# A two-layer perceiver block: the second query product moved behind the first scores, and two low parts of the experts exchanged

## The chip, the core and the metric

The kernel runs on one core of one Trainium2 chip. The time is that of one execution on the device in microseconds, from the first to the last instruction with what lies around them; of several runs the median counts.

## What is computed

Input are x (4 blocks of 128 rows, width 512) and a context (4 × 2048 rows, width 512). Six stages follow one another, each adding its result to x after a layer norm of its input:

```
x = x + cross attention, layer 0 (norm(x), ctx, ctx, mask)     # 16 heads of 32
x = x + retention, layer 0
x = x + experts, layer 0                                       # 8 experts, the best 2 of each row
x = x + norm(cross attention, layer 1 (norm(x), ctx, ctx))     # 16 heads of 32, no mask
x = x + gated recurrence, layer 1
x = x + experts, layer 1: 8 experts, the best 2 of each row:
        down(silu(gate(x)) * up(x)), weighted by the softmax of the two router values
```

The change touches cross attention (both layers use one function) and the experts of layer 1. In cross attention, q = norm(x) Wq + bq, k = ctx Wk + bk, v = ctx Wv + bv, scores = q k / sqrt(32) (where the mask hides a column, it counts as −1e9), softmax over the 2048 keys, times v, times Wo.

## The kernel before

**Cross attention, `stage_cross`.** All 512 queries (4 blocks of 128) are projected once, turned: product o (`project_q(o)`, L356) gives the 128 columns of q that belong to 4 heads, for all 512 rows, in one PSUM bank, `QB[o]`. It is a product in float32, from `wqT` (Wq, which lies in the tile `pt`) and `xT`. VectorE (`keep_q`, L578) adds the bias, in layer 0 also multiplies by a tile that clears fully hidden rows (four instructions), and splits the result into a high part `qhi` and a low part `qlo`; the semaphore `q_done` counts finished query blocks. Keys and values come in 16 groups of 512 keys: `project_k(g, o)` and `project_v(g, n)` use three products each of high and low parts (`three_products`, L91 to L95). Input of a group is split by ScalarE (`chi`, `high_part`) and GpSimd (`clo`, `low_part` L292).

Work is cut into 64 units u of four heads and one group: `scores(u)` (L399, twelve matmuls into the four banks S), maxima on VectorE (`max_of`: L605 with mask, L608 without), exponentials on ScalarE (L813), transposes of the probabilities (`turn_p`, L414, into two banks TB), copies to `pt`, and `outputs` (L431, into the bank `OB`) two units later. Keys and values run two units ahead. The order of each engine is written out by hand. Of TensorE's it is, ahead of the units:

```
v(0,0) v(0,1) turn_x k(0,0) [turn the mask's tile, layer 0] q(0) k(0,1) q(1)
unit 0: scores(0) q(2) v(0,2) q(3) k(0,2)      unit 1: scores(1) v(0,3) turn_p(0,0..1) k(0,3) turn_p(0,2..3)
```

VectorE's is `keep_q(0)`, `low_k(0, 1)`, `keep_q(1)`, then the four maxima of unit 0, `keep_q(2)`, `keep_q(3)`, the low part of k(0,2). The scores of unit 0 wait for two query blocks (`max(u + 1, 2)`, L405), though they read one. GpSimd starts on the second group's low parts when two query blocks are done (L315), and SyncE's load of the next group follows these. The bank OB is first written by the outputs of unit 0, in unit 2.

**Experts of layer 1, `stage_experts` with `layer` 1.** Rows are sorted into 15 tiles of 128 rows of one expert. Each tile g needs three weight matrices of 1 MB (kinds 0 gate, 1 up, 2 down) that SyncE loads into four slots in the order gate g, up g, down g − 1 (`load`, L1442). A slot is free once the low part of what was in it is made (`lo_done`). ScalarE makes the high part of a matrix (`high`, L1727), VectorE the low part (`low`, L1902 to L1905, 128 × 2048 elements). Rows of a tile are turned by TensorE (`turn_x`), their high part `xThi` made by ScalarE (`high_x`, L1740), the low part `xTlo` by VectorE (`low_x`, L1995). The gate product `expand(GB, 0, g)` (L1650) waits for `lo_done[0]` and `xlo_done` of its tile. Per pass g, the orders are:

```
TensorE: gate(g)  turn_h(g-1)  turn_x(g+1)  up(g)  contract(g-1)
ScalarE: silu(g)  high part of h(g-1)  high(gate, g+1)  high_x(g+1)  high(up, g+1)  high(down, g)  keep output
VectorE: low part of h(g-1)  low_x(g+1)  low(gate, g+1)  silu * up (g)  low(up, g+1)  low(down, g)
```

A wait in the text is a wait on a semaphore; an engine runs its instructions in order, so what is behind a waiting one waits too.

Of the kernel before, what the change touches and what calls it, by code (L numbers as in the profile page):

```python
# [27 lines left out]
C = D // P  # L28
# [146 lines left out]
def stage_cross(nc, k, name, t, L, x, x_in, mask, norm, prefetch):  # L175
# [19 lines left out]
    with ExitStack() as ctx:  # L195
# [34 lines left out]
        q_made, q_done, x_ready = sem("q_made"), sem("q_done"), sem("x_ready")  # L230
# [8 lines left out]
        S, TB, OB, KV = ps[0:4], ps[4:6], ps[6], ps[7]  # L239
        QB = (S[2], S[3], OB, TB[1])  # L240
        HALF = C * D // 2
# [12 lines left out]
        with nc.Block() as block:  # L254
# [35 lines left out]
            def _(pool):  # L290
# [23 lines left out]

                pool.wait_ge(q_done, 2)  # L315
                for c in range(C):
# [3 lines left out]
                for u in range(U + 2):  # L320
# [4 lines left out]
                    g = u // C  # L325
# [22 lines left out]
            def _(pe):  # L348
# [7 lines left out]
                def project_q(o):  # L356
                    pe.wait_ge(xT_done, C)
                    pe.wait_ge(wq_in, 16)
                    if o == 3:
                        pe.wait_ge(q_done, 1)  # L360
                        pe.wait_ge(v_done, 2)
                    for c in range(C):
                        last = pe.matmul(QB[o][:], wqT[:, c, o * P:(o + 1) * P], xT[:, c, :], start=(c == 0), stop=(c == C - 1))
                    last.then_inc(q_made, 1)
# [34 lines left out]
                def scores(u):  # L399

                    g, o = u // C, u % C
                    b = g // NCH
                    pe.wait_ge(klo_done, C * g + o + 1)
                    if u < C:
                        pe.wait_ge(q_done, max(u + 1, 2))  # L405
                    after(pe, exp_done, HPT * u)
                    for i, (q_part, k_part) in enumerate(((qhi, khi), (qhi, klo), (qlo, khi))):
                        for h in range(HPT):
                            rows = slice(h * HD, (h + 1) * HD)
                            ins = pe.matmul(S[h][:], q_part[rows, o, b * P:(b + 1) * P], k_part[rows, g % 2, o, :],  # L410
                                            start=(i == 0), stop=(i == 2))
                            if i == 2:
                                ins.then_inc(s_made, 1)

                def turn_p(u, n):
# [3 lines left out]
                    if u == 0 and n == 0:  # L419
                        pe.wait_ge(v_done, 2)  # L420
                    if u == 0 and n == 1:
                        pe.wait_ge(q_done, C)
# [8 lines left out]
                def outputs(u):  # L431
# [5 lines left out]
                    if u == 0:  # L437
                        pe.wait_ge(q_done, C - 1)
                    after(pe, oc_done, u)
# [54 lines left out]
                project_k(0, 1)  # L494
                project_q(1)
                for u in range(U + 2):
                    g, o = (u + C - LAG) // C, (u + C - LAG) % C
                    ahead = g < G
                    if u < U:
                        scores(u)  # L500
                    if u == 0:
                        project_q(2)
                    if 2 <= u < U + 2:
# [27 lines left out]
            def _(dve):  # L531
# [174 lines left out]
                low_k(0, 1)  # L706
                keep_q(1)
                if masked:
                    dve.wait_ge(hidden_done, 1)
                for u in range(U + 2):  # L710
# [5 lines left out]
                    if u == 0:  # L716
                        keep_q(2)
                        keep_q(3)
                    if u == U:
# [602 lines left out]
def stage_experts(nc, k, name, t, x, x_out, xg, od, layer, prefetch):  # L1322
# [30 lines left out]
    with ExitStack() as ctx:  # L1353
# [84 lines left out]
        with nc.Block() as block:  # L1438
# [440 lines left out]
            def _(dve):  # L1879
# [179 lines left out]
                else:  # L2059
                    for g in range(NG + 1):  # L2060
                        if g >= 1:
                            dve.wait_ge(hhi_done, g)
                            nc.vector.tensor_tensor(hlo[:, (g - 1) % 2, :], TB[0][:], f32(hhi[:, (g - 1) % 2, :]), ALU.subtract) \
                                .then_inc(hlo_done, 1)
                        if 1 <= g < NT - 1:
                            low_x(g + 1)
                        if g + 1 < NG:
                            low(0, g + 1)
                        if g < NG:
# [351 lines left out]
```

## Time and profile before

| what | value |
|---|---|
| three runs | 2252.75, 2248.92, 2246.71 us, median 2248.92 |
| the profiled execution | 2253.44 us |
| its span, first to last instruction | 2251.7 us |
| mean granted clock of TensorE | 0.969 |
| busy: TensorE, VectorE, ScalarE, GpSimd | 2120.6, 1410.6, 1376.8, 296.0 us |
| cross attention of layer 0 and of layer 1, about | 0 to 655 us, 1330 to 1970 us |
| experts of layer 1, about | 2058 us to the end |

The profile is one execution. Its page gives busy time of the engines and the costliest groups of instructions; its trace gives each instruction with start and length, what ended the idle time before it, and windows with busy time, granted clock and use of the DMA engines. Matmuls are pipelined: one starts before the one before it has ended, so the distance of two starts, not the length, is what one costs.

### The profile page before, as it was taken

What the parts mean: (1) busy time and instruction counts of PE and PEld (TensorE: products, weight loads), DVE (VectorE), ACT (ScalarE), POOL (GpSimd) and SP (SyncE); (2) the same over time, 40 slices, a digit from 0 to 9 for tenths busy, and PEclk for the clock granted to TensorE, in tenths of its full rate; (3) what the DMA queues carried; (4) which work ended last, traced back from release to release, by engine and by line L of the source; (5) the groups of instructions that cost most, each with busy time, mean ns of one, the idle gap of its engine ahead of it and who ended that gap; (6) DMA issues with size and microseconds to landing.
All of it is one profiled execution on the core that took longest, in us unless ns stands there. A gap on an engine that the chain in (4) does not pass through costs nothing. (4 is left out here: it accounts for less than half of the span.)

```text
span 2251.7 us, 37885 instructions
## 1 busy us (share of the span) xinstructions
PE 2120.6 (94%) x14773; PEld 1635.5 (73%) x14773; DVE 1410.6 (63%) x2399; ACT 1376.8 (61%) x2644; POOL 296.0 (13%) x268
## 2 busy tenths in 40 slices
PE   6999999999988987799999989999999999977998
PEld 4777787777864655688888856777877787756776
DVE  5555455555554775499999954555455454577887
ACT  3666566566652543388888835665665666554774
POOL 1111112122110000100000201121111121101001
PEclk9999999999997998899999989999999999988999
DMA  4001001010103012599999930100101010012996
GB/s 159 20 20 39 20 22 37 20 38 20 39 20 147 1 38 97 213 366 373 365 358 359 370 107 20 39 20 21 37 20 39 20 39 20 20 57 97 357 360 242
DMA packets 53776, 262.07 MB, mean 116 GB/s; under 512 B 9560, under 2 KB 9944, under 8 KB 26976
## 3 DMA queue, kind: packets, MB, share of 16 engines
q1 hardware_dynamic: 47296, 244.45, 29.0%
q0 software_dynamic: 2560, 8.39, 1.1%
q10 hardware_dynamic: 3744, 6.82, 0.8%
q8 instruction: 119, 1.95, 0.4%
q14 instruction: 57, 0.47, 0.1%
HBM read 243.65 MB, written 15.99 MB: 115 GB/s over the span
## 5 line engine op out<-in xcount | busy, mean ns | idle before, releaser
L613 DVE COPY c_pt<-bank 128x512 f32<-128x512 f32 x256 | 177.1, 692 | 557.5 <-PE bank L428 557.4
L813 ACT ACTIVATE c_pr<-wide,c_nmax 128x512 f32<-128x512 f32 x512 | 349.3, 697 | 147.5 <-DVE c_nmax L605 76.8
L295 POOL TENSOR_TENSOR c_clo<-land,c_chi 128x512 fp32r<-128x512 f32 x120 | 154.5, 1290 | 1007.0 <-ACT c_chi L782 911.9
L428 PE MATMUL bank<-ident,c_pr 128*128 128x128 f32 x2048 | 268.1, 274 | 2.7 <-ACT c_pt L820 1.4
L428 PEld LDWEIGHTS bank<-ident,c_pr 128*128 128x128 f32 x2048 | 239.8, 141 | 37.1 <-DVE c_pt L613 2.3
L796 ACT ACTIVATE c_khi<-bank,c_cols 128x512 fp32r<-128x512 f32 x128 | 88.1, 688 | 252.2 <-PE bank L95 252.2
L93 PE MATMUL bank<-c_wv_hi,c_chi 128*128 128x512 f32 x512 | 217.7, 425 | 18.4 <-DVE c_clo L544 17.1
L93 PE MATMUL bank<-c_chi,c_wk_hi 128*128 128x512 f32 x512 | 214.0, 418 | 0.3 <-DVE c_wk_lo L536 0.2
L94 PE MATMUL bank<-c_wv_lo,c_chi 128*128 128x512 f32 x512 | 202.6, 396 | 0.0
L95 PE MATMUL bank<-c_chi,c_wk_lo 128*128 128x512 f32 x512 | 202.4, 395 | 0.0
L95 PE MATMUL bank<-c_wv_hi,c_clo 128*128 128x512 f32 x512 | 202.3, 395 | 0.0
L94 PE MATMUL bank<-c_clo,c_wk_hi 128*128 128x512 f32 x512 | 199.1, 389 | 0.0
L820 ACT COPY c_pt<-bank 128x512 f32<-128x512 f32 x256 | 150.5, 588 | 63.0 <-PE bank L428 62.8
L605 DVE CUSTOM_DVE_ANT_0 wide<-wide,land 128x512 f32<-128x512 f32 x256 | 169.1, 722 | 5.8 <-PE wide L410 5.4
L608 DVE TENSOR_REDUCE c_nmax<-wide 128x1 f32<-128x512 f32 x256 | 158.8, 682 | 4.9 <-PE wide L410 4.6
L1905 DVE TENSOR_TENSOR moe_wlo<-moe_hr,moe_whi 128x2048 fp32r<-128x2048 f32 x68 | 153.3, 2284 | 6.7 <-ACT moe_whi L1732 6.7
L93 PE MATMUL wide<-moe_whi,moe_xThi 128*128 128x512 f32 x360 | 144.3, 401 | 10.0 <-issue 4.8
L95 PE MATMUL wide<-moe_whi,moe_xTlo 128*128 128x512 f32 x360 | 141.9, 394 | 0.0
L93 PEld LDWEIGHTS bank<-c_wv_hi,c_chi 128*128 128x128 f32 x512 | 96.7, 189 | 62.1 <-issue 24.3
L94 PE MATMUL wide<-moe_wlo,moe_xThi 128*128 128x512 f32 x360 | 141.6, 393 | 0.0
L444 PE MATMUL bank<-c_pt,c_v 128*32 128x128 f32 x4096 | 139.7, 278 | 1.6 <-ACT c_pt L820 1.6
L444 PEld LDWEIGHTS bank<-c_pt,c_v 128*32 128x32 f32 x4096 | 105.2, 110 | 49.5 <-issue 47.3
(416 smaller groups left out, 4270.1 us busy)
## 6 DMA issues: line engine op xcount, KB each, us to landing
moe_hr<-in_L_ffn_w SPq DMA_DIRECT2D x68, 1024.0 KB, 7.5
land<-in_L_ffn_w SPq DMA_DIRECT2D x34, 1024.0 KB, 7.8
land<-in_ctx SPq DMA_DIRECT2D x31, 1024.0 KB, 4.9
moe_raw<-in_L_ffn_w SPq DMA_DIRECT2D x18, 1024.0 KB, 7.8
moe_raw<-in_L_ffn_we_gate SPq DMA_DIRECT2D x8, 1024.0 KB, 6.8
land<-in_L_ffn_we_up SPq DMA_DIRECT2D x8, 1024.0 KB, 6.6
moe_raw<-in_L_ffn_we_down SPq DMA_DIRECT2D x8, 1024.0 KB, 6.7
moe_raw<-in_L_ffn_we_up SPq DMA_DIRECT2D x7, 1024.0 KB, 7.4
```

Of the source, the lines that this page charges most:

```text
L93: pe.matmul(out, w_hi, m_hi, start=start, stop=False, skip_group_check=not check)
L94: pe.matmul(out, w_hi, m_lo, start=False, stop=False, skip_group_check=not check)
L95: return pe.matmul(out, w_lo, m_hi, start=False, stop=stop, skip_group_check=not check)
L295: nc.gpsimd.tensor_tensor(clo[:, g % 2, c, :], raw[:, c, :], f32(chi[:, g % 2, c, :]), ALU.subtract) \
L428: last = pe.transpose(TB[n % 2][:, h * P:(h + 1) * P], pr[:, u % 2, h, n * P:(n + 1) * P], k["ident"][:])
L444: last = pe.matmul(OB[h * HD:(h + 1) * HD, 0:P], v[:, (T4 * g + n) % VR, at:at + HD], pt[:, n, h * P:(h + 1) * P], start=(n == 0), stop=(n ...
L605: nc.vector.tensor_tensor_reduce(S[h][:], S[h][:], hidden[:, i * CH:(i + 1) * CH], -1.0, BIG, ALU.add, ALU.min, into).then_inc(max_done, 1)
L608: nc.vector.tensor_reduce(into, S[h][:], AX.X, ALU.max, negate=True).then_inc(max_done, 1)
L613: nc.vector.tensor_copy(pt[:, n, :], TB[0][:]).then_inc(pt_dve, 1)
L813: nc.scalar.activation(pr[:, u % 2, h, :], S[h][:], ACT.Exp, bias=nmax[:, b % 2, i, at:at + 1], scale=-1.0 if masked else 1.0, accum_out=d ...
L820: nc.scalar.copy(pt[:, n, :], TB[1][:]).then_inc(pt_act, 1)
L1905: nc.vector.tensor_tensor(wlo[kind][:, g % 2, :], raw[n % RW], f32(whi[kind][:, g % 2, :]), ALU.subtract).then_inc(lo_done[kind], 1)
```

## The change

In `stage_cross`: product 1 of the queries goes behind the scores of unit 0 on TensorE, and its VectorE work behind the maxima of unit 0. Scores of unit 0, and GpSimd's first low parts, wait for one query block instead of two. The banks of the products become S[2], OB, TB[1], TB[0] in place of S[2], S[3], OB, TB[1]. The waits that go with the banks move: products 1 to 3 wait for one query block and the first two value blocks, the transposes of unit 0 for all four query blocks already at the first, the outputs of unit 0 for two blocks instead of three. In `stage_experts`, layer 1: in passes 1 to 13, VectorE makes the low part of the next gate weights ahead of that of the next rows.

```diff
--- before.py
+++ after.py
@@ -237,7 +237,7 @@
         done, acc_scaled, early_scaled, early_joined, late_joined = (sem(s) for s in ("done", "acc_scaled", "early_scaled", "early_joined", "late_joined"))
         ps = k["ps"]
         S, TB, OB, KV = ps[0:4], ps[4:6], ps[6], ps[7]
-        QB = (S[2], S[3], OB, TB[1])
+        QB = (S[2], OB, TB[1], TB[0])
         HALF = C * D // 2
         FIRST = 2 if x_in is not None else 1
         landings = list(k["landings"])
@@ -312,7 +312,7 @@
                     pool.wait_ge(scaled, 2 * n + 2)
                     nc.gpsimd.tensor_tensor(acc[:, b % 2, :], acc[:, b % 2, :], part[:, i % 2, :], ALU.add).then_inc(joined, 1)
 
-                pool.wait_ge(q_done, 2)
+                pool.wait_ge(q_done, 1)
                 for c in range(C):
                     low_part(1, c)
                 pool.wait_ge(q_done, C)
@@ -356,7 +356,7 @@
                 def project_q(o):
                     pe.wait_ge(xT_done, C)
                     pe.wait_ge(wq_in, 16)
-                    if o == 3:
+                    if o > 0:
                         pe.wait_ge(q_done, 1)
                         pe.wait_ge(v_done, 2)
                     for c in range(C):
@@ -402,7 +402,7 @@
                     b = g // NCH
                     pe.wait_ge(klo_done, C * g + o + 1)
                     if u < C:
-                        pe.wait_ge(q_done, max(u + 1, 2))
+                        pe.wait_ge(q_done, u + 1)
                     after(pe, exp_done, HPT * u)
                     for i, (q_part, k_part) in enumerate(((qhi, khi), (qhi, klo), (qlo, khi))):
                         for h in range(HPT):
@@ -417,8 +417,6 @@
                     if n == 0:
                         pe.wait_ge(exp_done, HPT * u + HPT)
                     if u == 0 and n == 0:
-                        pe.wait_ge(v_done, 2)
-                    if u == 0 and n == 1:
                         pe.wait_ge(q_done, C)
                     if n % 2 == 0:
                         after(pe, pt_dve, 2 * u + n // 2)
@@ -435,7 +433,7 @@
                     pe.wait_ge(pt_act, 2 * u + 2)
                     pe.wait_ge(v_done, T4 * g + T4)
                     if u == 0:
-                        pe.wait_ge(q_done, C - 1)
+                        pe.wait_ge(q_done, 2)
                     after(pe, oc_done, u)
                     after(pe, aT_done, C * finished(TURN, u + 2))
                     for n in range(T4):
@@ -492,13 +490,13 @@
                     pe.transpose(TB[1][:, 0:P], manyr, k["ident"][:]).then_inc(any_turned, 1)
                 project_q(0)
                 project_k(0, 1)
-                project_q(1)
                 for u in range(U + 2):
                     g, o = (u + C - LAG) // C, (u + C - LAG) % C
                     ahead = g < G
                     if u < U:
                         scores(u)
                     if u == 0:
+                        project_q(1)
                         project_q(2)
                     if 2 <= u < U + 2:
                         outputs(u - 2)
@@ -704,7 +702,6 @@
                     s.then(nc.vector.tensor_copy(manyT, TB[1][:, 0:P]))
                 keep_q(0)
                 low_k(0, 1)
-                keep_q(1)
                 if masked:
                     dve.wait_ge(hidden_done, 1)
                 for u in range(U + 2):
@@ -714,8 +711,8 @@
                         for h in range(HPT):
                             max_of(u, h)
                     if u == 0:
-                        keep_q(2)
-                        keep_q(3)
+                        for c in range(1, C):
+                            keep_q(c)
                     if u == U:
                         fold_max(G - 1)
                     if o == 2 and u > C and 0 < (g - 1) % NCH and g < G:
@@ -2062,10 +2059,10 @@
                             dve.wait_ge(hhi_done, g)
                             nc.vector.tensor_tensor(hlo[:, (g - 1) % 2, :], TB[0][:], f32(hhi[:, (g - 1) % 2, :]), ALU.subtract) \
                                 .then_inc(hlo_done, 1)
+                        if g + 1 < NG:
+                            low(0, g + 1)
                         if 1 <= g < NT - 1:
                             low_x(g + 1)
-                        if g + 1 < NG:
-                            low(0, g + 1)
                         if g < NG:
                             dve.wait_ge(up_made, g + 1)
                             dve.wait_ge(silu_done, g + 1)
```

## Rows read from the trace of the kernel before

**Rows 1.** The page: TensorE over the span, and VectorE's masked maxima

```profile
PE 2120.6 (94%) x14773; PEld 1635.5 (73%) x14773; DVE 1410.6 (63%) x2399; ACT 1376.8 (61%) x2644; POOL 296.0 (13%) x268
...
L605 DVE CUSTOM_DVE_ANT_0 wide<-wide,land 128x512 f32<-128x512 f32 x256 | 169.1, 722 | 5.8 <-PE wide L410 5.4
```

**Rows 2.** Windows, layer 0's attention: length, busy PE, PEld, DVE, ACT, POOL, clock, DMA

```profile
57.00:200.00 143.00, 142.61 (x1270) 113.90 (x1273) 75.34 (x193) 88.40 (x210) 29.60 (x24) 1.00 0.07 23
```

**Rows 3.** Timeline of TensorE, layer 0: start us, length us, engine, line, instruction

```profile
32.45 3.60 PE L363 MATMUL wide<-c_pr,c_pt 128*128 128x512 f32 x8
39.17 0.80 PE L410 MATMUL wide<-c_khi,c_qhi 32*128 32x512 f32 x4 [3.12 <-DVE c_qlo L587]
...
40.75 6.09 PE L363 MATMUL bank<-c_pr,c_pt 128*128 128x512 f32 x8
46.28 0.80 PE L93 MATMUL bank<-c_wv_hi,c_chi 128*128 128x512 f32 x1
...
49.43 3.59 PE L363 MATMUL bank<-c_pr,c_pt 128*128 128x512 f32 x8
52.46 0.79 PE L93 MATMUL bank<-c_chi,c_wk_hi 128*128 128x512 f32 x1
```

**Rows 4.** Timeline of VectorE, layer 0

```profile
32.16 0.69 DVE L587 TENSOR_TENSOR c_qlo<-c_v,c_qhi 128x512 fp32r<-128x512 f32 x1
...
38.33 0.69 DVE L587 TENSOR_TENSOR c_qlo<-c_v,c_qhi 128x512 fp32r<-128x512 f32 x1
```

**Rows 5.** Timeline of TensorE, head of layer 1's attention

```profile
1349.47 3.59 PE L363 MATMUL wide<-c_pr,c_pt 128*128 128x512 f32 x8
1355.26 0.51 PE L410 MATMUL wide<-c_khi,c_qhi 32*128 32x512 f32 x4 [2.20 <-DVE c_qlo L587]
...
1356.16 5.40 PE L363 MATMUL bank<-c_pr,c_pt 128*128 128x512 f32 x8
1361.00 0.79 PE L93 MATMUL bank<-c_wv_hi,c_chi 128*128 128x512 f32 x1
```

**Rows 6.** Timeline of VectorE, head of layer 1's attention

```profile
1348.26 0.69 DVE L587 TENSOR_TENSOR c_qlo<-c_v,c_qhi 128x512 fp32r<-128x512 f32 x1
```

**Rows 7.** Windows of 1 us, head of layer 0's attention

```profile
43.00:44.00 1.00, 1.00 (x2) 0.34 (x1) 0.64 (x2) 1.00 (x5) 1.00 (x1) 0.50 0.00 0
```

**Rows 8.** Timeline of GpSimd, layer 0

```profile
39.11 4.96 POOL L295 TENSOR_TENSOR c_clo<-land,c_chi 128x512 fp32r<-128x512 f32 x4 [37.42 <-DVE c_qlo L587]
```

**Rows 9.** Timeline of TensorE, experts of layer 1

```profile
2093.48 0.47 PE L93 MATMUL wide<-moe_whi,moe_xThi 128*128 128x512 f32 x1 [0.62 <-DVE moe_xTlo L1997]
...
2193.95 0.39 PE L95 MATMUL bank<-moe_whi,moe_hlo 128*128 128x512 f32 x1
2194.45 0.47 PE L93 MATMUL wide<-moe_whi,moe_xThi 128*128 128x512 f32 x1
...
2222.71 0.47 PE L93 MATMUL wide<-moe_whi,moe_xThi 128*128 128x512 f32 x1
```

**Rows 10.** Timeline of VectorE, experts of layer 1

```profile
2191.45 0.69 DVE L1997 TENSOR_TENSOR moe_xTlo<-bank,moe_xThi 128x512 fp32r<-128x512 f32 x1 [0.93 <-ACT moe_xThi L1740]
2192.06 2.28 DVE L1905 TENSOR_TENSOR moe_wlo<-moe_raw,moe_whi 128x2048 fp32r<-128x2048 f32 x1
```

**Rows 11.** Timeline of ScalarE, experts of layer 1

```profile
2189.01 1.94 ACT L1732 CAST moe_whi<-moe_raw 128x2048 fp32r<-128x2048 f32 x1
2190.82 0.60 ACT L1740 CAST moe_xThi<-bank 128x512 fp32r<-128x512 f32 x1
```

**Rows 12.** Waits in the experts of layer 1: us in total, times, longest us

```profile
DVE moe_xTlo L1997 <- ACT moe_xThi L1740: 17.8, 15, 2.7
...
PE wide L93 <- issue: 3.1, 3, 1.5
PE wide L93 <- DVE moe_wlo L1905: 2.2, 1, 2.2
```

**Rows 13.** Windows of 2 us, experts of layer 1 (columns as in rows 2)

```profile
2114.00:2116.00 2.00, 2.00 (x9) 1.63 (x10) 2.00 (x2) 2.00 (x2) 0.00 (x0) 1.00 0.64 164
```

## The prediction

> **What bounds the kernel now.** I read the page first: TensorE is busy for 94% of the span and no other engine for more than 63% [rows 1]. That is a mean, so I went to the stretches in which the changed lines run. In the body of an attention stage TensorE is busy 142.61 of 143 us at full clock and VectorE 75.34 [rows 2]: there TensorE alone sets the time, and whatever its queue reaches earlier stays won until the stage ends. The head of the stage is different. The timeline of TensorE [rows 3] shows a hole: the second query product starts at 32.45, and then the engine stands idle 3.12 us until the first scores start at 39.17. VectorE's timeline [rows 4] names the cause: the low part of the second query block (start 38.33, 0.69 long) ends at 39.02, and the scores wait for two blocks though unit 0 reads only the first, which was ready at 32.85. The third query product, right behind the hole, takes from 40.75 to 46.28, 5.53 us, where the fourth takes 3.03 (49.43 to 52.46). A look at the granted clock says why: 0.50 in that stretch [rows 7], the lower of TensorE's two levels, 1.2 instead of 2.4 GHz. So the hole is paid twice. Layer 1 repeats it, smaller (no mask): idle 2.20, then a product of 4.84 us [rows 5].
>
> In the experts of layer 1 TensorE is again nearly always busy, but three engines form a ring. From the gate product at 2194.45 to that at 2222.71 there are three periods in 28.26 us, 9.42 each [rows 9], and the gap ahead of the gate product is 2194.45 − 2193.95 = 0.50 us where a matmul elsewhere in the run follows after 0.23: some 0.25 us of idle per tile. What ends it is VectorE's low part of the gate weights (2192.06, 2.28 long, ends 2194.34) [rows 10]. Ahead of that VectorE sat 0.93 us idle for the high part of the next rows, though ScalarE had the high part of the weights ready earlier (2189.01 + 1.94 = 2190.95) than that of the rows (2190.82 + 0.60 = 2191.42) [rows 11]. This wait occurs 15 times, 17.8 us in all [rows 12].
>
> **Part 1, attention, both layers.** Nothing is added or removed in arithmetic: four query products (eight TensorE passes each) and their four sets of VectorE instructions stay. The scores of unit 0 move ahead of query product 1 and wait for one query block; product 1 goes into the outputs' bank, products 2 and 3 into two banks of the transposes. Sum, layer 0, from 32.45 to the start of the value product that was at 46.28. Before: 13.83 us. After: wait for the first query block, 32.85 plus the hand-over of 0.15 seen in 39.02 to 39.17, gives a start at 33.00, so 0.55; scores at full clock 0.90 (1355.26 to 1356.16 [rows 5]); two query products at 3.03, 6.06. Together 7.51, a saving of 6.3 us. It holds only if TensorE keeps its full clock through 0.55 us of idle; TensorE's longest such spell among the experts, 1.5 us [rows 12], ends at 2113.87, and the granted clock right after it is 1.00 [rows 13], so I take it. With the third product still at the low clock it would be 2.5 us less.
>
> Layer 1, from 1349.47 to 1361.00. Before: 11.53 us. The first query block is complete at 1348.26 + 0.69 = 1348.95 [rows 6], so there is no wait; scores 0.90 and two products 6.06 make 6.96. Saving 4.6 us.
>
> The value product, product 3 and the key product that follow keep their order and lengths, and from scores of unit 1 on nothing changes. Their waits, with layer 0's new times: scores of unit 1 would start near 49.4 and want query block 1. Its product (3.60 us long, from 33.9) ends at 37.5, and a masked block was ready 2.97 us after its product's end (39.02 against 32.45 + 3.60 = 36.05), so it is there by 40.5. The first maxima (four at 0.72 [rows 1], from about 34.1 to 37.0) now lie on VectorE ahead of block 1, inside the time in which it used to wait for the product. The exponentials follow the maxima one by one and are long done. The new wait of the transposes for all four query blocks (block 3: its product from 43.2 to 46.8, ready at 49.7) is met two microseconds before the transposes of unit 0 are reached, which stand behind scores and a value product. Queued behind product 1's added wait are product 2 and the value product; the wait is for the first query block, which the scores ahead of it have already awaited, so it costs nothing. The outputs' bank is not used by anyone before unit 0's outputs, two units later.
>
> GpSimd's four low parts of the next keys' input took 4.96 us from 39.11 [rows 8] and now start when ScalarE's high parts exist, about 34; the one DMA of SyncE behind them (the next input) is issued some 5 us earlier. Nobody waits for either for tens of microseconds. But the four now lie beside VectorE's instructions on query block 1 instead of beside the maxima. The trace has no such pair; bounds are 0 and all of GpSimd's 4.96 us added to VectorE. Block 1 would then be ready at 45.5, block 2 at 48.5, block 3 at 51.4 instead of 49.7, and the key's low part behind it, which TensorE wants at about 50.9, some 1.2 us late. I take 0, since the slack ahead covers most of it. The Trainium skill, "SBUF — State Buffer", section "Who interferes with whom", states that an operation of GpSimd and one of VectorE with two SBUF inputs exclude each other for the whole instruction. By it the sum would move towards that 1.2 us, and no row of this trace tests it.
>
> Attention together: 10.9 us, bounds 7.2 (the third product at the low clock in layer 0, and the 1.2) and 11.4 (if the 0.55 wait is hidden too).
>
> **Part 2, experts of layer 1.** Two VectorE instructions change places in each pass from the second to the fourteenth: low part of the gate weights (2.28 us) ahead of low part of the next rows (0.69). Both are needed by the next gate product, so the end of the pair counts. Before, the pair starts when ScalarE's second copy is there (2191.42); after, when the first is (2190.95): 0.47 us earlier, and 2.28 us later the rows' copy is long there. The pair can't come out later than before: its length is the same, and ScalarE makes the two in the new order. How much of 0.47 counts per pass? Where TensorE's gap is 0.25, only 0.25; then TensorE is the bound (9.42 − 0.25 = 9.2 us of work, against 9.42 − 0.47 = 8.95 for the ring). From the gate product at 2093.48 to that at 2222.71 there are 13 periods in 129.2 us; at 9.2 each they would be 119.6. So 9.6 us is the ceiling, and most of it sits in four long periods whose idle (3.1 us over three, and 2.2 once [rows 12]) comes through late weight transfers.
>
> For those a second effect matters: SyncE issues the load of the next up weights when the gate weights' low part is done, and that moves 0.47 + 0.69 = 1.16 us earlier. The DMA engines do run dry for moments (busy share 0.64 and 164 GB/s at 2114 to 2116 [rows 13]), so earlier issue fills some of this. Bounds: 0.5 us (only the last long period's pair counts, since everything ahead of it is absorbed by the transfer it waits for) and 9.6. The nearest rows are the regular periods: the eighth is the last long one, and six after it at 0.25 make 1.5; plus 0.5 at that one; plus up to 1 us for earlier loads. I take 3.0.
>
> **Sum.** 10.9 + 3.0 = 13.9 us. The profiled execution took 2253.44 us (span 2251.7): 2239.5. It lay 4.5 above the median 2248.92, so the forecast is 2235.0 us, −0.62%.
>
> **Rivals.**
> (A) The experts' reorder is hidden by transfers. For it: long periods end with a DMA, and the engines of the DMA are nearly full. Against it: the regular periods wait for no DMA. Gain 10.9 to 11.4: 2238.
> (B) The experts' ring loosens more than taken, the long periods shrinking with the earlier loads, and the 2.2 us idle no longer lowers the clock: gain 10.9 + 6 to 8, 2231. Against it: the DMA share is near 1 for most of the stretch.
> (C) TensorE drops its clock in the head of unit 0 all the same, or VectorE becomes late there: gain 7.2 in attention, with 0 to 3 from the experts, 2239 to 2242. Against it: no idle over 0.6 us is left there.
> (D) The saving is taken back in attention by a wait that is now hidden, such as the bank of values and keys or the value copies. It would have to be within two units, since then TensorE is full [rows 2]. I find none in rows 3 and 4; with half of the attention's gain gone and nothing from the experts, 5.4: 2243.5, within 0.3%.
> (E) Slower. All that follows unit 0 runs 6.3 us, later 10.9 us, earlier against a clock control that may not follow the kernel. The mean granted clock of 0.969 means about 2251.7 × 0.031 × 2 = 140 us at half clock, mostly in short stretches between stages where TensorE idles. Each microsecond more of it costs at most a half. To cancel 13.9 us it takes 28 us more of these, to be slower by 0.3% (6.7 us) 41 us more; that is where it decides. It gives 2256 or more. Against it: idle spells there stay as they are, and some stretches would shorten as others lengthen. The Trainium skill, "TensorE: Matmul & The Clock Gate", Part 1, says the activity watch is free-running, so that one kernel shows different counts of slow matmuls from run to run; this trace can't show that, a comparison of two could.
> (F) The change doesn't do what it says: if product 1 in the outputs' bank waited for something else, the idle would stay. The code gives it only waits that scores have met. Same time, 2249; folded into the chance of D.
>
> **Chances.** Forecast 0.62, A 0.13, B 0.10, C 0.06, D and F 0.07, E 0.02. A measurement tells about 0.3% (6.7 us) from no change. Faster by more: forecast, A, B, C less 0.02 of C: 0.89; within: 0.09; slower: 0.02. Range: B's 2231 and C's 2242, with some 3 us on both sides for the spread of the runs shown (2246.71 to 2252.75): 2228 to 2243.
>
> **What would show it.** Layer 0: scores of unit 0 near 33.0 on TensorE, no idle over 0.6 us until scores of unit 1 near 49.4, granted clock 1.00 between 33 and 49; in layer 1 the same 4.6 us earlier than before within the stage. Then identical unit periods. Experts: no wait of VectorE's rows' low part for ScalarE; instead a short one (about 0.5 us) of the weights' low part for ScalarE's weights copy; regular periods of 9.2 instead of 9.42 us. Wrong would be: a half-clock stretch within 33 to 49; regular periods still 9.42; or a stage other than these three that has changed by over 2 us.

## The result, and the profile after

The changed kernel took 2232.37 us (median of 18 runs, 2221.37 to 2241.96), the kernel before 2246.86 in the 18 runs beside them (2237.2 to 2252.75). The ratio is 0.9945, 95% interval [0.993, 0.9959]: faster by 0.55%, against a forecast of 2235.0 us within 2228 to 2243. The profiled execution of after has a span of 2240.3 us, 11.4 less than that of before.

The head of layer 0's attention on TensorE, after (start us, length us, engine, line, instruction, idle before it and what ended it). It answers to [rows 3].

```profile
32.98 0.50 PE L410 MATMUL wide<-c_khi,c_qhi 32*128 32x512 f32 x4 [0.41 <-DVE c_qlo L585]
...
33.88 7.13 PE L363 MATMUL bank<-c_pr,c_pt 128*128 128x512 f32 x16
40.45 0.79 PE L93 MATMUL bank<-c_wv_hi,c_chi 128*128 128x512 f32 x1
...
49.84 0.51 PE L410 MATMUL wide<-c_khi,c_qhi 32*128 32x512 f32 x4
...
51.47 0.50 PE L93 MATMUL bank<-c_wv_hi,c_chi 128*128 128x512 f32 x1 [0.66 <-DVE c_klo L589]
```

The scores of unit 0 start at 32.98 behind 0.41 us of idle, not at 39.17 behind 3.12. The two query products stand in one row (16 passes), the value product follows at 40.45 (before: 46.28) and there is no idle until 51.47, where the key's low part holds TensorE for 0.66 us as it did before. The windows answer to [rows 7]: length, then busy time (and instructions) of PE, PEld, DVE, ACT and POOL, granted clock, DMA share, GB/s.

```profile
32.00:52.00 20.00, 18.94 (x77) 10.68 (x76) 14.19 (x36) 8.10 (x16) 4.96 (x4) 1.00 0.16 54
...
57.00:200.00 143.00, 143.00 (x1278) 114.28 (x1277) 74.80 (x192) 89.19 (x212) 29.96 (x25) 1.00 0.07 23
```

The clock stays at 1.00 (2.4 GHz) all through the head, and the body of the stage is as full as in [rows 2]. VectorE and GpSimd in the same head, after; the first answers to [rows 4], the second to [rows 8].

```profile
38.47 1.21 DVE L581 TENSOR_TENSOR c_v<-c_v,c_aT 128x128 f32<-128x128 f32 x4
...
40.18 0.69 DVE L585 TENSOR_TENSOR c_qlo<-c_v,c_qhi 128x512 fp32r<-128x512 f32 x1
...
41.91 0.90 DVE L581 TENSOR_TENSOR c_v<-c_v,c_aT 128x128 f32<-128x128 f32 x4
...
49.47 0.69 DVE L585 TENSOR_TENSOR c_qlo<-c_v,c_qhi 128x512 fp32r<-128x512 f32 x1
```

```profile
33.96 4.96 POOL L295 TENSOR_TENSOR c_clo<-land,c_chi 128x512 fp32r<-128x512 f32 x4 [32.28 <-ACT c_chi L779]
```

Query block 1 is ready at 40.18 + 0.69 = 40.87, block 3 at 50.16. The forecast had 40.5 and 49.7. GpSimd works until 33.96 + 4.96 = 38.92, so most of it still lies beside the maxima and only its last 0.45 us beside VectorE's four mask multiplications, which take 1.21 us instead of 0.90, 0.31 more.

The head of layer 1's attention on TensorE, after; it answers to [rows 5].

```profile
1345.96 0.51 PE L410 MATMUL wide<-c_khi,c_qhi 32*128 32x512 f32 x4
...
1346.87 7.13 PE L363 MATMUL bank<-c_pr,c_pt 128*128 128x512 f32 x16
1353.44 0.79 PE L93 MATMUL bank<-c_wv_hi,c_chi 128*128 128x512 f32 x1
```

From the place of [rows 5]'s first row to the value product it was 11.53 us; now it is 1353.44 − 1345.96 = 7.48, 4.05 less. Counted from the first query product (1343.30 before, 1339.71 after) the head is 13.73 us instead of 17.70, 3.97 less.

The experts of layer 1. TensorE's gate products (2084.84 and 2211.27 answer to 2093.48 and 2222.71 of [rows 9]), then the waits of VectorE, TensorE and ScalarE in this stage, which answer to [rows 12] (us in total, times, longest us), and last three waits of the kernel before: VectorE's for the weights' high part and ScalarE's for down weights.

```profile
2084.84 0.47 PE L93 MATMUL wide<-moe_whi,moe_xThi 128*128 128x512 f32 x1 [0.62 <-DVE moe_xTlo L1994]
```

```profile
2202.06 0.47 PE L93 MATMUL wide<-moe_whi,moe_xThi 128*128 128x512 f32 x1 [0.43 <-DVE moe_xTlo L1994]
...
2211.27 0.39 PE L93 MATMUL wide<-moe_whi,moe_xThi 128*128 128x512 f32 x1
```

```profile
DVE moe_wlo L1902 <- ACT moe_whi L1729: 18.1, 19, 2.4
...
DVE moe_xTlo L1994 <- ACT moe_xThi L1737: 1.6, 2, 1.4
...
PE wide L93 <- DVE moe_xTlo L1994: 7.2, 7, 2.0
...
ACT moe_whi L1729 <- DMA land<-in_L_ffn_we_down: 9.0, 7, 2.6
...
ACT moe_whi L1729 <- DMA moe_raw<-in_L_ffn_we_down: 6.1, 5, 1.8
...
ACT moe_xT L1850 <- ACT moe_ob L1868: 2.3, 5, 0.5
```

```profile
DVE moe_wlo L1905 <- ACT moe_whi L1732: 3.9, 3, 2.4
...
ACT moe_whi L1732 <- DMA land<-in_L_ffn_we_down: 6.2, 6, 1.9
ACT moe_whi L1732 <- DMA moe_raw<-in_L_ffn_we_down: 3.8, 6, 1.0
```

VectorE's wait of the rows' low part is nearly gone (17.8 us to 1.6), but the one ahead of the weights' low part grew from 3.9 to 18.1: together 21.7 before and 19.7 after, so the wait was moved more than removed. Thirteen periods, 2084.84 to 2211.27, take 126.43 us against 129.23. ScalarE waits 9.0 + 6.1 = 15.1 us for down weights; before it was 10.0.

**Where the 11.4 us lie.** TensorE's rows of after are earlier than their partners of before by 5.83 us at layer 0's value product (46.28 to 40.45), by only 3.51 at the head of layer 1's attention (1349.47 to 1345.96), by 7.56 at its end (1361.00 to 1353.44), 8.64 at a gate product near the experts' start (2093.48 to 2084.84) and 11.44 at the last one (2222.71 to 2211.27). So the heads gave 5.83 and 4.05, the experts 2.80; between the two heads 2.3 us went back, in code that the change doesn't touch, and 1.1 came in the untouched stretch after layer 1's head. Most of the 2.3 went in the last products of layer 0's experts. Their start and the start of the product that follows them, and a window of 20 us there (columns as above), before and then after:

```profile
1304.96 1.12 PE L1635 MATMUL wide<-moe_b,moe_xn 8*128 8x512 f32 x2
...
1321.93 1.98 PE L1636 MATMUL wide<-moe_ob,moe_xn 128*128 128x512 f32 x4 [0.84 <-DVE moe_ob L2003]
```

```profile
1300.00:1320.00 20.00, 19.25 (x44) 8.50 (x43) 9.58 (x12) 2.94 (x5) 0.00 (x0) 0.74 0.00 0
```

```profile
1299.15 1.12 PE L1632 MATMUL wide<-moe_b,moe_xn 8*128 8x512 f32 x2
...
1317.70 1.98 PE L1633 MATMUL wide<-moe_ob,moe_xn 128*128 128x512 f32 x4 [0.84 <-DVE moe_ob L2000]
```

```profile
1300.00:1320.00 20.00, 19.16 (x33) 7.84 (x33) 6.52 (x11) 0.42 (x1) 0.00 (x0) 0.66 0.00 0
```

The mean granted clock is 0.74 in before, (1 − 0.74) × 20 × 2 = 10.4 us at the lower of the two levels, and 0.66 in after, 13.6 us. At 1.2 GHz half of the time is lost, so the 3.2 us more cost up to 1.6 us, and that is what the rows show: 1321.93 − 1304.96 = 16.97 us became 1317.70 − 1299.15 = 18.55. Another 0.64 us went between layer 1's first value product and its first query product (13.02 us instead of 12.38), where the low clock lasted longer too. So which of these microseconds belong to the change has to come from experiments.

### The profile page after: what moved, and what is told of

It reads as the page before. It is cut to its first block and busy times, and to the rows that moved or that the text cites. A ratio compares the mean times of both kernels' runs of the same rounds, so it can differ in the third digit from the quotient of the medians.

```text
span 2240.3 us, 37889 instructions
## 1 busy us (share of the span) xinstructions
PE 2113.9 (94%) x14773; PEld 1632.3 (73%) x14773; DVE 1412.5 (63%) x2399; ACT 1377.0 (61%) x2644; POOL 295.9 (13%) x268
```

## The experiments

**Each part alone.** `attn_only` is the kernel after with the experts' order of before; `experts_only` is the kernel before with one edit:

```diff
-                        if 1 <= g < NT - 1:
-                            low_x(g + 1)
                         if g + 1 < NG:
                             low(0, g + 1)
+                        if 1 <= g < NT - 1:
+                            low_x(g + 1)
```

> Only the attention part of the change; VectorE's order in the experts as before. Theory (both parts add, attention carries most): 10 us faster than before, ratio 0.9955; in the trace layer 0's value product of unit 0 starts 5.8 us earlier than before, and layer 1's head gives 4 us more, as in the changed kernel; the experts of layer 1 take what they took before (139.2 us from gate product 0 or 1, 129.2 us over 13 periods, with regular periods of 9.42). Rival (the experts' reorder carries a large part of the 14 us): no more than 7 us faster.

Measured: 0.9959 [0.994, 0.9978] (median 2234.91 of 12 runs, 2246.36 for before), so 9.2 us. The heads on TensorE are those of after: 14.23 us from the first query product to the value product in layer 0, 13.73 in layer 1. The experts, which were to take 129.2 us over thirteen periods, took 126.01.

> Only VectorE's exchange in the experts of layer 1. Theory: 1 to 3 us faster, ratio 0.9987 to 0.9995, hardly to be told from no change by the clock on the wall; in the trace 13 periods of the experts take 126.5 us (129.2 before), VectorE's wait for the rows' high part is gone and one for the weights' high part of 0.5 to 0.9 us per tile is there. Rival (the loop is bound by the weight transfers, and the 2.8 us seen in the changed kernel came from a half-clock stretch that happened to be missing): 13 periods between 128 and 130 us.

Measured: 0.9993 [0.9977, 1.0009] (2242.42, 12 runs): 1.6 us, and the interval includes no change. The product of the two ratios is 0.9952, and after has 0.9945, which agrees with two parts that add up. Most of the gain is attention's. The thirteen gate periods took 129.38 us in the trace of `experts_only`: not the 126.5 of the theory, but inside the rival's 128 to 130. `attn_only` keeps the old order and has 126.01, so two traces of one order (129.23 and 126.01) differ by more than the 2.80 us between before and after, and the full kernels don't show a gain in the experts.

**The same kernel once more.** `after_again` has no edit.

> The changed kernel once more, for its spread and a second trace. Expected: ratio 0.9945 as before, head of layer 0 5.85 us shorter again to 0.1 us; in the experts the sum of the 13 periods between 125 and 128 us if the exchange is worth 3 us by itself, up to 129 if transfers and half-clock stretches set it at random.

Measured: 0.9943 [0.9921, 0.9965] (2231.65, 6 runs). Its thirteen periods took 127.56 us, 1.1 more than those of after; layer 0's value product starts at 40.45 again.

**Fill the hole.** The prediction says the hole in layer 0 is paid twice, the idle and then the low clock. `fill_idle` is the kernel before with more work in the hole, an extra query product whose result isn't used:

```diff
                 project_q(1)
+                for c in range(C):
+                    pe.matmul(OB[:], wqT[:, c, 0:P], xT[:, c, :], start=(c == 0), stop=(c == C - 1))
```

> The kernel before, with TensorE kept busy in the hole: the second query product (with the first block's weights) is computed once more into the outputs' bank, which nobody uses yet, right behind product 1; its result is never read. Theory (the hole is paid twice, by idle and by the half clock behind it): the extra product of 3.0 us fits into the 3.7 us hole, so scores of unit 0 start where they did, about 39.2, but scores take 0.9 instead of 1.6 and the third product 3.0 instead of 5.5 us: value product at 43.1 instead of 46.3, and in layer 1, where the hole is 2.8 us, the scores 0.3 later and the third product 3.0 instead of 4.8, 1.5 us won. Together 4 to 4.7 us faster than before with more work. Rival (the slow third product is slowed by GpSimd's work beside it, not by the clock): third product still 5.5 and 4.8 us, time 0.3 us longer than before.

TensorE in the head of layer 0 in `fill_idle`:

```profile
32.42 3.59 PE L363 MATMUL wide<-c_pr,c_pt 128*128 128x512 f32 x8
35.85 3.60 PE L497 MATMUL bank<-c_pr,c_pt 128*128 128x512 f32 x8
39.37 0.50 PE L410 MATMUL wide<-c_khi,c_qhi 32*128 32x512 f32 x4
...
40.27 3.70 PE L363 MATMUL bank<-c_pr,c_pt 128*128 128x512 f32 x8
43.41 0.80 PE L93 MATMUL bank<-c_wv_hi,c_chi 128*128 128x512 f32 x1
```

Measured: 0.9982 [0.9956, 1.0009], 4.0 us, with an interval that includes none. The rows are clearer than the time. The scores start at 39.37 with no idle ahead (before: 39.17 behind 3.12 us), and the third query product takes 43.41 − 40.27 = 3.14 us instead of 5.53, with GpSimd's four low parts still beside it (39.08 to 44.06). A kernel with eight more passes reaches its value product 2.9 us sooner (43.41 against 46.28; by heads 1.4 less than the quickest of the old order, below). So the low clock comes with the idle and goes with it, and GpSimd beside the product does not cause it. In layer 1 the third product takes 3.14 us too, instead of 4.84, but the win over the head is 0.5 us (17.17 against 17.70): the extra product costs 3.43 us (35.85 − 32.42 in the rows above), and the hole there is only 2.20 [rows 5]. The expectation had sized the product at 3.0 and the hole at 2.8.

**GpSimd beside VectorE.** `gpsimd_late` is the kernel after with `pool.wait_ge(q_done, 1)` as 2, so that GpSimd's four low parts start when block 1 is done.

> The changed kernel, but GpSimd's first low parts wait for two query blocks again, so that they don't lie beside VectorE's instructions on block 1. Theory (exclusion between the two engines costs the 0.31 us by which the four mask multiplications grew, hidden by slack): the four multiplications take 0.90 instead of 1.21 us, everything on TensorE in the head starts where it starts in the changed kernel, value product of unit 0 at 40.45. Rival (it costs time on the path): TensorE's head is earlier by 0.3 us.

GpSimd, and VectorE on query blocks 1 to 3, in `gpsimd_late`:

```profile
40.65 5.11 POOL L295 TENSOR_TENSOR c_clo<-land,c_chi 128x512 fp32r<-128x512 f32 x4 [38.96 <-DVE c_qlo L585]
```

```profile
38.48 0.90 DVE L581 TENSOR_TENSOR c_v<-c_v,c_aT 128x128 f32<-128x128 f32 x4
...
41.91 4.19 DVE L581 TENSOR_TENSOR c_v<-c_v,c_aT 128x128 f32<-128x128 f32 x4
...
49.49 0.69 DVE L585 TENSOR_TENSOR c_qlo<-c_v,c_qhi 128x512 fp32r<-128x512 f32 x1
```

Measured: 2238.58 us in one run, inside the spread of after. On block 1 the mask multiplications are back at 0.90, but now those of block 2 lie beside GpSimd and take 4.19 instead of 0.90, from 41.91 to 46.10, just past GpSimd's end at 40.65 + 5.11 = 45.76. Blocks 2 and 3 are read late enough (block 3 ready at 50.18, after: 50.16) and TensorE's head is unchanged. This is the collision that the prediction had to bound without a row: 0.31 us in the place where the change puts it, 3.29 if the whole of it falls on the multiplications. The Trainium skill, "SBUF — State Buffer", section "Who interferes with whom", has a VectorE operation with two SBUF inputs and one of GpSimd that reads SBUF exclude each other for the whole instruction. The 4.19 agrees with that: in the 3.85 us beside GpSimd the four multiplications lost 3.29.

**Down weights at half their size.** The experts' periods in after (9.2 us and more) could be held by late down weights. `half_down_old` (on before) and `half_down_new` (on after) load only half of each down matrix after the first tile, so a sixth of the weight transfer is left out and the output is not the block's; the instructions are otherwise the same.

```diff
-                    sp.dma_start(raw[n % RW], src).then_inc(raw_in[n % RW], 16)
+                    if not first and kind == 2 and g > 0:
+                        sp.dma_start(raw[n % RW][:, 0:C * D // 2], src[:, 0:C * D // 2]).then_inc(raw_in[n % RW], 16)
+                    else:
+                        sp.dma_start(raw[n % RW], src).then_inc(raw_in[n % RW], 16)
```

> The kernel before with only the first half of each down weight matrix loaded (from the second tile on) in the experts of layer 1; the rest of the slot holds older data. It leaves out a sixth of the weight transfer. Theory (VectorE's old order sets the regular period, transfers the long ones): regular periods stay 9.42 us, long ones go; 13 periods take 123 us. Rival (transfers set all): periods of 9.2 us, 120 us.

> The changed kernel with the same half loads of the down weights in the experts of layer 1, a sixth of the weight transfer left out. Theory (the exchange is worth 0.25 us per tile, and the changed kernel doesn't show it because the down weights come late and hold ScalarE): all periods 9.2 us, 13 of them 120 us, 3 us less than with the old order and the same loads; ScalarE's waits for down weights gone. Rival (the exchange buys nothing, with or without transfers): 123 us, periods 9.4.

The larger of ScalarE's two rows of waits for down weights in `half_down_new` (the other is 0.4 us), then two neighbouring gate products of it and two of `half_down_old`:

```profile
ACT moe_whi L1732 <- DMA moe_raw<-in_L_ffn_we_down: 2.0, 2, 1.0
```

```profile
2192.68 0.39 PE L93 MATMUL wide<-moe_whi,moe_xThi 128*128 128x512 f32 x1
...
2201.79 0.39 PE L93 MATMUL wide<-moe_whi,moe_xThi 128*128 128x512 f32 x1
```

```profile
2188.82 0.47 PE L93 MATMUL wide<-moe_whi,moe_xThi 128*128 128x512 f32 x1
...
2198.25 0.47 PE L93 MATMUL wide<-moe_whi,moe_xThi 128*128 128x512 f32 x1
```

The old order still needs 9.43 us per period (2198.25 − 2188.82) with down weights that hardly anyone waits for, the new one 9.11 (2201.79 − 2192.68), 0.32 less or 4.2 over thirteen. Thirteen periods took 124.14 us old and 121.13 new, each 1.1 more than its theory, because two long periods stayed. Only the waits for down weights went (15.1 us in after, 2.4 here); those for gate and up weights did not shrink (4.6 and 5.0). `half_old_again` and `half_new_again` repeat both.

> Old order of VectorE, half loads of the down weights (a sixth of the weight transfer left out), once more. Theory: 13 periods within 0.7 us of 124.14, regular ones 9.43 us. Rival (the 3 us between the orders was chance): as near to 121 as to 124.

> New order of VectorE, half loads of the down weights (a sixth of the weight transfer left out), once more. Theory: 13 periods within 0.7 us of 121.13, regular ones 9.05 to 9.2 us. Rival: as near to 124 as to 121.

They gave 125.50 and 120.25, both outside the 0.7 us that the expectations allowed, but apart in the same way: the new order is better by 3.0 and 5.3 us, 4.1 in the mean. With full loads the old order has 129.23, 126.01 and 128.71 (mean 128.0), the new one 126.43, 127.56, 129.38 and 126.25 (mean 127.4). A part of that scatter is the clock. In the thirteen periods of the kernels with full loads, the granted clock fell behind six of the seven spells of 1.9 to 2.5 us in which TensorE stood idle ahead of a gate product (two of them in `experts_only`; the exception is that of `attn_only`, 2.47 us) and behind none of up to 1.7 us. Where it did not fall, the old order took 126.0 us and the new one 126.4 and 126.3; with one fall, 129.2 and 128.7 against 127.6. With half loads it fell nowhere in these periods. So the reorder makes the ring shorter, by some 4 us, and with full loads, as far as these few traces go, late down weights take most or all of it away. Each of the four had one run: 2248.02 and 2234.41 us old, 2232.74 and 2224.34 new; they differ by the clock elsewhere too (below), and only the periods are read here.

**The output copy first.** In after ScalarE waits for the down weights with the copy of finished outputs, the SiLU and the gate weights queued behind it. `output_first` moves the copy and its store ahead of the conversion of the down weights:

```diff
+                        # wait out_made, copy to moe_ob, store(g - 1)
                         if g < NG:
                             high(2, g)
-                        # wait out_made, copy to moe_ob, store(g - 1)
```

> The changed kernel, and in the experts of layer 1 ScalarE keeps and stores the output of a tile ahead of the high part of the down weights instead of behind it. Theory (with the exchange in place the ring that binds is: down weights late, ScalarE held in front of them, output copy and silu behind): silu no longer follows the output copy with the 0.46 us hand-over, 13 periods take 124 to 125.5 us against 126.2 to 127.6 in three traces of the changed order, 1 to 2 us faster than the changed kernel, ratio 0.994. Rival (the transfers themselves set the pace, whatever ScalarE's order): 126 to 128 us, no gain.

Measured: 0.9926 [0.9902, 0.995] (2231.17, 6 runs), thirteen periods 125.00 us in one trace, with one fall of the clock in them, the last five 9.09 to 9.11 where after has 9.2 to 9.6. That is the period of the half loads with all weights loaded, so what held the late periods of after was ScalarE standing in front of the down weights, not the amount of data. It has the best ratio of the full kernels, 4 us below after's, but the two intervals overlap, so the gain in time is not shown. `out_first_half` joins it with the half loads.

> The same with only the first half of each down weight matrix loaded from the second tile on (a sixth of the weight transfer left out). Theory: once transfers don't hold ScalarE its order has nothing to give, 121 us for 13 periods as with the changed order and half loads (121.13). Rival (the output copy is on the ring by itself): below 120.

Measured: 2232.28 us in one run, thirteen periods 121.28, as in `half_down_new`. With the weights early the place of the output copy made no difference in this trace.

## Why the prediction was right, and where it was not

**Layer 0's head: right, 0.5 us less than forecast.** The steps came as written: scores at 32.98 (33.00 foreseen), full clock through the idle, 0.90 for the scores, no idle before scores of unit 1 at 49.84. The support for the full clock was misread: 1.5 us is not TensorE's longest idle among the experts, [rows 12] has one of 2.2 behind which the clock fell (below); the 0.4 us that came is far from either. The term that was mis-sized is the two query products at 3.03 each. They take 40.45 − 33.88 = 6.57. The 3.03 was read where fp32r products of values or keys stand on both sides. With another float32 product behind it a product takes 3.43 (32.42 to 35.85 in `fill_idle`), 0.40 more, and one behind the scores 3.14 (40.27 to 43.41), 0.11 more: 2 × 3.03 + 0.40 + 0.11 = 6.57. Saving 5.83 where 6.3 stood.

**Layer 1's head: the same.** 7.48 instead of 6.96, saving 4.05 where 4.6 stood. Attention together gave 9.9 us in the profiled pair and 9.2 by the ratio of `attn_only`, with 10.9 taken and 7.2 to 11.4 as bounds. The low clock of the third product, whose return was rival C, came in no trace of the new order: from the first query product to the value product there are 14.22 to 14.24 us in layer 0 in all eight traces of it. The old order gave 20.04 in before and 19.78, 18.67 and 18.59 in other traces of it, behind the same idle. The scores' row behind the hole, in `half_down_old` and in `half_old_again`, which are one program:

```profile
39.10 0.80 PE L410 MATMUL wide<-c_khi,c_qhi 32*128 32x512 f32 x4 [3.12 <-DVE c_qlo L587]
```

```profile
39.16 0.51 PE L410 MATMUL wide<-c_khi,c_qhi 32*128 32x512 f32 x4 [3.12 <-DVE c_qlo L587]
```

Once the first scores already run at the low clock (0.80), once at full clock (0.51). So the profiled execution of before had one of the dearer heads, and against a head of 18.6 the saving is 4.4, not 5.8. The mean over the four traces of the old order is 19.27 us in layer 0 and 17.65 in layer 1, so the saving is 5.0 and 3.9, together 9.0, which fits the 9.2 of `attn_only`.

**GpSimd beside VectorE: bounded too widely.** The prediction put the four low parts beside block 1 "instead of beside the maxima" and bounded them by all of 4.96 us. By its own times (from about 34, block 1 from 37.5) they overlap block 1 by 1.5 us at most; 0.31 us was lost, and nobody waited for it.

**Experts: wrong step.** The sentence that failed is "the regular periods wait for no DMA". In four of the last five periods of before ScalarE did wait for down weights, 0.16 to 0.59 us, but it cost nothing, because the SiLU behind them then waited 1.3 to 1.7 us for TensorE anyway. ScalarE in one of these periods:

```profile
2193.39 1.90 ACT L1732 CAST moe_whi<-land 128x2048 fp32r<-128x2048 f32 x1 [0.16 <-DMA land<-in_L_ffn_we_down]
...
2197.50 0.60 ACT L1853 ACTIVATE moe_xT<-wide 128x512 f32<-128x512 f32 x1 [1.72 <-PE wide L95]
```

With VectorE's 0.93 us moved the ring is fast enough to meet the down weights, and that slack is used up: ScalarE's wait for them grew from 10.0 us to 15.1, 15.1 in `after_again`, 14.4 in `experts_only` and 15.6 in `gpsimd_late`, while the other traces of the old order with full loads have 9.9 (`fill_idle`) and 6.9 (`attn_only`). One turn of the ring in after, ScalarE, then VectorE, between the gate products at 2192.42 and 2202.06:

```profile
2193.25 1.92 ACT L1729 CAST moe_whi<-moe_raw 128x2048 fp32r<-128x2048 f32 x1 [1.81 <-DMA moe_raw<-in_L_ffn_we_down]
2195.07 0.58 ACT L1868 COPY moe_ob<-bank 128x512 f32<-128x512 f32 x1
...
2196.10 0.60 ACT L1850 ACTIVATE moe_xT<-wide 128x512 f32<-128x512 f32 x1 [0.46 <-ACT moe_ob L1868]
...
2197.07 1.92 ACT L1729 CAST moe_whi<-land 128x2048 fp32r<-128x2048 f32 x1
```

```profile
2199.02 2.29 DVE L1902 TENSOR_TENSOR moe_wlo<-land,moe_whi 128x2048 fp32r<-128x2048 f32 x1 [0.93 <-ACT moe_whi L1729]
2201.23 0.68 DVE L1994 TENSOR_TENSOR moe_xTlo<-bank,moe_xThi 128x512 fp32r<-128x512 f32 x1
```

The down weights land 1.81 us late, at 2193.25. Behind their conversion stand the output copy, the issue of its store (0.33 us, the only thing in the 0.46 us of idle), then the SiLU, which now follows that copy and not TensorE, the gate weights' high part (2197.07 + 1.92 = 2198.99), VectorE's low part of them (2199.02) and of the rows, which ends at 2201.91. TensorE starts the gate product at 2202.06 behind 0.43 us of idle, and this period is 9.64 us. TensorE's idle ahead of the gate products is the same in all, 7.4 us before and 7.2 after. Rival A, "hidden by transfers", was the truer one for this part, and its gain of 10.9 to 11.4 us in all is near what the two parts gave alone. The forecast of 3.0 us met 2.8 in the profiled pair by chance. Period by period the pair differs by −1.2 to +1.7 us; the sixth to the eighth together took 32.0 us before and 29.9 after, 2.1 of the 2.8, and in before they hold an idle of 2.24 us with a stretch at the low clock behind it, (1 − 0.86) × 12 × 2 = 3.4 us, which costs up to 1.7 us. The window, before:

```profile
2160.00:2172.00 12.00, 9.76 (x41) 7.71 (x40) 8.58 (x6) 8.65 (x9) 0.00 (x0) 0.86 0.94 363
```

Of what should show it, the short wait of the weights' low part was 0.95 us each (18.1 over 19) and not 0.5, and the last five periods took 9.21 to 9.64 us and not 9.2. The 3.0 itself held small slips: five regular periods follow the last long one, not six. And the gain of one regular period, 0.25 us in the sum, was 0.32 where the weights came early.

**The sum.** 13.9 us stood, 14.5 is the difference of the medians, 2246.86 × 0.0055 = 12.4 that of the ratio, 9.2 + 1.6 = 10.8 that of the parts measured alone, each with an interval of ± 3 to 4 us. Attention's 9 us are shown by the rows of its heads and by a run of its own. The experts' share is not told from nothing by any run with full loads: the interval of `experts_only` reaches from 2 us slower to 5 us faster. So the total is right with one term 2 us too high and another that holds by chance.

**The clock (rival E).** Its size was right, and which way it goes is open each time. The mean granted clock and span of two executions of one program, `half_down_old` and `half_old_again`:

```profile
core 0: 2246.1 us, clock 0.969
```

```profile
core 0: 2232.5 us, clock 0.978
```

The low-clock time is 2246.1 × 0.031 × 2 = 139 us in one and 2232.5 × 0.022 × 2 = 98 in the other; the spans differ by 13.6 us, as much as the change brings. The code is the same, so this is no effect of any edit. From layer 0's first value product in unit 0 to layer 1's first query product, where no experiment changes TensorE's order, the thirteen traces have 1284.0 to 1299.3 us (before 1297.0, after 1299.3), and the two executions of this one program 1296.8 and 1284.0. The prediction counted "a stage other than these three that has changed by over 2 us" among the signs of being wrong. It came, 2.3 us, and by these traces it says nothing about the change: the same stretch moves by 12.7 us with no edit at all. That is also why the 11.4 us of one pair of traces agree with the medians only loosely. The Trainium skill, "TensorE: Matmul & The Clock Gate", Part 1, calls the activity watch free-running and expects different counts of slow matmuls from one kernel; these two executions agree with that.

**Slower, D and F** didn't come: the outputs' bank made nobody wait, and within two units TensorE was full.

## What to carry to other kernels

A wait at the head of a stage whose body is bound by TensorE is worth its idle plus the low-clock stretch that may follow it; look for a consumer that waits for more than it reads, and put other products between. Before pricing the removal of one wait in a ring of three engines, look for what is next latest (here weights that landed with little to spare), because a ring that turns faster meets it. And where untouched stages move by more than an edit is worth, read its gain inside its own stage and in several traces, not from one pair of spans.

## What the runs showed of the hardware that was not expected

A float32 product of eight passes took 3.43 us at 2.4 GHz from its start to that of the next float32 product, and 3.03 to that of an fp32r value or key product, so its price depends on its neighbours. The same 3.12 us of idle at the same place cost a head of 18.6 or of 20.0 us; the 0.4 us that is left in the new order was followed by full clock in all eight traces of it. In the head of layer 1, 2.2 us of idle came with a stretch at 1.2 GHz in all four traces of the old order. Among the experts 2.47 us of idle did in one trace (`fill_idle`) and not in another (`attn_only`), and the 1.97 to 2.28 us ahead of the very first gate product did in none of nine. So the length of an idle spell alone did not tell whether the clock fell. VectorE's four 128x128 multiplications with both inputs in SBUF took 0.90 us alone, 1.21 beside the tail of GpSimd's work and 4.19 beside the whole of it.
